# Q and K of the first band from rounded part and remainder, attention output per band, and a new order on all engines, in a fused window-attention block

## The reference

```python
h = roll(ln(x, g1, b1), (-3, -3), axis=(1, 2))
q, k, v = heads(window_partition(h) @ w_qkv + b_qkv)
attn = softmax(q * 32**-0.5 @ k.T + bias[rel_index] + shift_mask)
x = x + roll(window_reverse((attn @ v) @ w_proj + b_proj), (3, 3), axis=(1, 2))
return x + gelu(ln(x, g2, b2) @ w_fc1 + b_fc1) @ w_fc2 + b_fc2     # exact gelu
```

## Time and profile before

| | us |
|---|---|
| median of the three timed runs | 3138.68 |
| the profiled execution | 3140.98 |
| span of its trace, first to last instruction | 3139.2 |
| TensorE matmuls busy | 2989.0 (95%) |
| VectorE busy | 2907.3 (93%) |
| ScalarE busy | 2255.3 (72%) |
| GpSimd busy | 1385.2 (44%) |

### The profile page before, as it was taken

One profiled execution on the slowest core, in us unless ns is written; L12 is line 12 of the kernel. 1 busy time (PEld: TensorE's weight loads), 2 busy tenths in 40 slices (PEclk: granted clock), 3 DMA queues, 4 the chain that ended last, 5 costly groups with the idle time before them and its releaser, 6 DMA issues.

```text
span 3139.2 us, 119115 instructions
## 1 busy us (share of the span) xinstructions
PE 2989.0 (95%) x51984; PEld 2732.5 (87%) x51984; DVE 2907.3 (93%) x7463; ACT 2255.3 (72%) x4480; POOL 1385.2 (44%) x775
## 2 busy tenths in 40 slices
PE   5999999999999999999999999999999999999998
PEld 3888888988888888889888888988888898888887
DVE  7999999999999999999999999999999999999995
ACT  3777777777777777777777777777777777777775
POOL 2444444444444444444444444444444444444442
PEclk9999999999999999999999999999999999999999
DMA  1111111111111111111111111111111111111110
GB/s 54 33 33 33 33 43 33 33 40 37 33 35 42 33 33 33 44 33 33 40 37 33 33 43 34 33 33 44 33 33 42 35 33 33 40 36 34 33 28 22
DMA packets 217571, 111.78 MB, mean 36 GB/s; under 512 B 15095, under 2 KB 216791, under 8 KB 217047
## 3 DMA queue, kind: packets, MB, share of 16 engines
q1 hardware_dynamic: 216899, 104.14, 13.0%
q10 hardware_dynamic: 147, 0.02, 0.0%
HBM read 52.73 MB, written 51.38 MB: 33 GB/s over the span
## 4 chain that ended last, share of the span: by engine, by line
PE 59%; DVE 29%; ACT 9%; issue 3%; SPq 0%; DMA 0%; POOL 0%; POOLq 0%; DVEq 0%; ACTq 0%
PE psum L767 13%; PE psum L725 7%; DVE xn L556 7%; PE psum L692 6%; PE psum L727 5%; PE psum L726 5%; DVE scores L576 5%; PE psum L699 4%; PE psum L746 4%; PE psum L753 4%; PE psum L707 3%; PE psum L720 3%; PE psum L732 3%; ACT probs L356 3%; DVE stream L590 3%
## 5 line engine op out<-in xcount | busy, mean ns | idle before, releaser
L318 POOL TENSOR_TENSOR rstd<-ve,minus_half 112x7 f32<-112x7 f32 x256 | 380.3, 1486 | 1251.7 <-DVE ve L551 1251.7
L767 PE MATMUL psum<-wfc,hT 128*112 128x128 f32 x7168 | 803.5, 273 | 1.5 <-ACT hT L410 1.5
L767 PEld LDWEIGHTS psum<-wfc,hT 128*112 128x112 f32 x7168 | 791.2, 177 | 2.1 <-issue 2.1
L410 ACT ACTIVATE hT<-psum,bias_h 128x392 f32<-128x392 f32 x1024 | 573.7, 599 | 233.0 <-PE psum L727 232.9
L314 POOL TENSOR_TENSOR probs<-probs,row_inv 128x784 f32<-128x784 f32 x256 | 383.7, 1521 | 470.7 <-DVE row_inv L585 470.7
L576 DVE TENSOR_TENSOR scores<-scores,row_max 128x784 f32<-128x784 f32 x256 | 447.5, 1748 | 8.8
L725 PE MATMUL psum<-x2T_hi,wfc_hi 128*128 128x392 f32 x1024 | 405.6, 396 | 28.0 <-DVE stream L590 25.8
L590 DVE TENSOR_TENSOR stream<-psum,stream 112x384 f32<-112x384 f32 (+1 forms) x512 | 303.9, 602 | 97.2 <-PE psum L753 83.3
L556 DVE TENSOR_SCALAR xn<-stream,mean,rstd 112x128 f32<-112x128 f32 x896 | 375.4, 476 | 1.6 <-POOL rstd L318 1.6
L321 POOL TENSOR_TENSOR stream<-stream,brow_fc 112x896 f32<-112x896 f32 x128 | 360.3, 2815 | 5.6 <-DVE xn L556 5.6
L402 ACT ACTIVATE kT<-psum,bias_k 128x392 f32<-128x392 f32 x256 | 150.8, 589 | 289.0 <-PE psum L732 285.6
(11 more groups left out here) (77 smaller groups left out, 5785.4 us busy)
## 6 DMA issues: line engine op xcount, KB each, us to landing
x_in<-in_x SPq DMA_DIRECT2D x224, 168.0 KB
out<-stream SPq DMA_DIRECT2D x224, 168.0 KB
x_in<-in_x SPq DMA_DIRECT2D x224, 17.5 KB
out<-stream SPq DMA_DIRECT2D x224, 17.5 KB
x_in<-in_x SPq DMA_DIRECT2D x224, 10.5 KB
out<-stream SPq DMA_DIRECT2D x224, 10.5 KB
x_in<-in_x SPq DMA_DIRECT2D x32, 96.0 KB
out<-stream SPq DMA_DIRECT2D x32, 96.0 KB
```

The costliest lines, as they stand in the source:

```text
L410: act.activation(hT[:, chunk, band * BAND:(band + 1) * BAND], tok_psum(c)[:, 0:BAND], ACT.Gelu, bias=bias_h[:, chunk:chunk + 1]).then_inc( ...
L767: last = pe.matmul(tok_psum(h)[0:TOK, (t - t0) * C:(t - t0 + 1) * C], hT[:, chunk, t * TOK:(t + 1) * TOK], wfc2[:, chunk, :], start=chunk ...
```

## The change

It touches three things.

1. Q and K of band 0 are computed like those of band 1, by `product` on `xT_hi` and `xT_lo`, which now hold both bands. So `round_x(k, 0)` on ScalarE and `split_x(k, 0)` on VectorE are new, once per step.
2. `attend` and `copy_o` are split by band, each with its own semaphore; the output of band b lies at columns b*196 of both qkvo banks. The banks of V, Q and K change.
3. The order in every `step` is rewritten, with the waits that go with it, and some work moves to another n.

```diff
-xT_hi = sb("xT_hi", [C, 1, BAND], F32R)
-xT_lo = sb("xT_lo", [C, 1, BAND], F32R)
+xT_hi = sb("xT_hi", [C, 2, BAND], F32R)
+xT_lo = sb("xT_lo", [C, 2, BAND], F32R)
-V_BANK, Q_BANK, K_BANK = (1, 1), (0, 0), (0, 0)
+V_BANK, Q_BANK, K_BANK = (1, 0), (0, 1), (1, 0)
-def o_psum(parity):
-    return psum[:, QKVO_BANK + parity, 0:BANDS * PAIRS * N]
+def o_psum(band, parity):
+    return psum[:, QKVO_BANK + parity, band * PAIRS * N:(band + 1) * PAIRS * N]
...
-        act.activation(xT_hi[:, 0, :].rearrange("c (w n) -> c w n", n=N),
...
-        hi, lo = (part[:, 0, :].rearrange("c (w n) -> c w n", n=N) for part in (xT_hi, xT_lo))
+        hi, lo = (part[:, band, :].rearrange("c (w n) -> c w n", n=N) for part in (xT_hi, xT_lo))
...
-def copy_o():
+def copy_o(band):
+    image = oT[:, :, band, :].rearrange("c i (a w j) -> c w a i j", w=2, j=WIN)
-        for band in range(BANDS):
-            made = o_psum(parity)[:, band * PAIRS * N:(band + 1) * PAIRS * N]
-            image = oT[:, :, band, :].rearrange("c i (a w j) -> c w a i j", w=2, j=WIN)
-            last = act.activation(image[:, parity, :, :, :],
-                                  made.rearrange("c (a i j) -> c a i j", i=WIN, j=WIN), ACT.Copy)
-    last.then_inc(o_copied, 1)
+        last = act.activation(image[:, parity, :, :, :],
+                              o_psum(band, parity).rearrange("c (a i j) -> c a i j", i=WIN, j=WIN), ACT.Copy)
+    last.then_inc(o_copied[band], 1)
...
-def attend():
-    for band in range(BANDS):
-        for pair in range(PAIRS):
-            cols = slice((band * PAIRS + pair) * N, (band * PAIRS + pair + 1) * N)
-            for parity in range(2):
-                keys = slice(HALF * parity, HALF * parity + N)
-                for h in range(HEADS):
-                    rows = slice(HD * h, HD * (h + 1))
-                    last = pe.matmul(o_psum(parity)[rows, cols], vs[keys, band, pair, rows],
-                                     probsT[keys, band, h // 2, pair, h % 2, 0:N], start=True, stop=True)
-    last.then_inc(o_made, 1)
+def attend(band):
+    for pair in range(PAIRS):
+        cols = slice(pair * N, (pair + 1) * N)
+        for parity in range(2):
+            keys = slice(HALF * parity, HALF * parity + N)
+            for h in range(HEADS):
+                rows = slice(HD * h, HD * (h + 1))
+                last = pe.matmul(o_psum(band, parity)[rows, cols], vs[keys, band, pair, rows],
+                                 probsT[keys, band, h // 2, pair, h % 2, 0:N], start=True, stop=True)
+    last.then_inc(o_made[band], 1)
 def product(made, w_hi, w_lo, x_hi, x_lo):
 def qk_product(k, bank, part, band):
-    if band == 0:
-        return pe.matmul(made, wqk[:, part, :], xT[:, k % 2, 0, :, 0:N], start=True, stop=True)
-    return product(made, wqk_hi[:, part, :], wqk_lo[:, part, :], xT_hi[:, 0, :],
-                   xT_lo[:, 0, :])
+    return product(made, wqk_hi[:, part, :], wqk_lo[:, part, :], xT_hi[:, band, :],
+                   xT_lo[:, band, :])
 def make_q(k, band):
```

More of the change, by code:

```diff
@@ L336, in step @@
                     normalise_probs(1)
[L337 to L346, removed]
             run_steps(step)
@@ L419, in step @@
                 if has(n - 1):
+                    wait(act, fc1_made[5], upto(n - 1))
+                    gelu(5)
+                    wait(act, fc1_made[6], upto(n - 1))
+                    gelu(6)
+                if has(n):
+                    wait(act, o_made[1], upto(n))
+                    copy_o(1)
+                    copy_o(0)
+                if has(n - 1):
+                    wait(act, fc1_made[1], upto(n - 1))
+                    gelu(1)
                     wait(act, fc1_made[0], upto(n - 1))
                     gelu(0)
[L422 to L433, removed]
                 if has(n + 1):
@@ L436, in step @@
                     copy_q(1)
-                if has(n - 1):
-                    wait(act, fc1_made[5], upto(n - 1))
-                    gelu(5)
+                if has(n + 2):
+                    wait(act, xT_made[1], upto(n + 2))
+                    copy_x(n + 2, 1)
                 if has(n + 1):
@@ L644, in step @@
                     shift_scores(n, 1)
+                    wait(dve, exp_done[0], upto(n))
+                    inverse_sums(n, 0)
                 if has(n - 1):
@@ new lines, in step @@
+                if has(n - 1):
+                    wait(pe, gelu_done[5], upto(n - 1))
+                    make_hidden(1)
+                    wait(pe, gelu_done[6], upto(n - 1))
+                    make_hidden(0)
+                if has(n + 1):
+                    wait(pe, o_copied[0], upto(n))
+                    if n < 0:
+                        wait(pe, xT_split[1], upto(n + 1))
+                    make_q(n + 1, 1)
+                if has(n):
+                    wait(pe, gelu_done[1], upto(n - 1))
+                    project(1)
+                    wait(pe, gelu_done[0], upto(n - 1))
@@ L775, in step @@
                     project(0)
-                if has(n - 1):
+                if has(n + 2):
                     wait(pe, residual_added[1], upto(n))
-                    if n >= steps:
-                        wait(pe, gelu_done[3], upto(n - 1))
-                    make_hidden(5)
+                    if n < 0:
+                        wait(pe, xn1_ready[1], upto(n + 2))
+                    transpose_tiles(xn1, 1, xT_made)
                 if has(n + 1):
-                    wait(pe, q_copied[1], upto(n + 1))
@@ L793, in step @@
                     make_scores(1)
+                if has(n - 1):
+                    wait(pe, gelu_done[3], upto(n - 1))
+                    make_hidden(7)
                 if has(n + 2):
@@ L800, in step @@
                     transpose_tiles(xn1, 0, xT_made)
-                    wait(pe, gelu_done[7], upto(n - 1))
-                    transpose_tiles(xn1, 1, xT_made)
                 if has(n + 1):
@@ L805, in step @@
                 if has(n - 1):
+                    wait(pe, gelu_done[7], upto(n - 1))
+                    make_out(1)
                     wait(pe, xT_copied[0], upto(n + 2))
[L807 to L808 removed]
                     make_out(0)
[L810 to L814 removed]
```

235 lines of the change are left out of this document (98 added, 137 removed).

## The result

The changed kernel takes 3169.89 us against 3139.05 in the same comparison: ratio 1.0095, 95% interval 1.0078 to 1.0113. It is slower by 1%. The forecast was 3058 us and faster, with a range up to 3150.

The account below looks back on a forecast made before the run. TensorE was taken to bound the kernel, VectorE just under: 23.16 us at the granted clock, 0.12 gap and 0.10 joints made 23.38 a step; 127 steps plus 90 us gave 3059, adjusted to 3058; range 3022 to 3150.

Parts of the forecast that it names:

- TensorE's part: TensorE's own list per step: 22.86 us before plus 0.14 for the new arithmetic, 23.00 us.
- The gap: Idle matmul time in attend at instruction packet borders: 0.68 us a step before, 0.12 forecast after.
- a divide in the time of the 256 instructions ahead: In attend, a packet border stops TensorE if the 256 instructions ahead passed in under about 2.2 us.
- VectorE's clean list: VectorE's step without GpSimd meetings: 19.98 us plus 0.55 for the new split; 20.9 with the projection wait.
- The wait between the projections: VectorE between the two projections: an unavoidable 0.4 us, as half 0 takes longer than the addition of half 1.
- the sum of VectorE's meetings with GpSimd: Time VectorE loses per step where GpSimd excludes it: 0.8 to 2.3 us, leaving VectorE just under TensorE.
- `normalise` xn2 against `normalise_probs`: VectorE's unbroken xn2 run beside GpSimd's normalise_probs 0: 0 to 1.5 us, taken as 0.
- the 0.7 for xn1: VectorE's normalise xn1 against GpSimd's two add_rows: 0.2 to 1.6 us, taken 0.7.
- rival (c): GpSimd takes turns between tiles of VectorE's xn1 and xn2 runs: slower, 24.7 us a step, 3227 us; chance 0.2.
- my three signs of being wrong: VectorE's busy share passes TensorE's; single L556 rows reach 2 us mid-run; the L720 gap keeps its 73 us.
- the powers: GpSimd's rstd power, started by the first mean_var, against the second's small VectorE operations: 0 to 1.48 us.
- Slack of 2.5 us over a step: VectorE, 20.9 against 23.4 us a step, can lose 2.5 us to GpSimd and waits before it binds.

Follow-up runs that it names:

- adds_late: The changed kernel with both GpSimd add_rows of a step waiting until VectorE has normalised xn1; 3023.54 us, ratio 0.9653 to the kernel before.
- before_adds_late: The kernel before, old order and arithmetic, with GpSimd's add_row for x waiting until band 0's scores are shifted; 3114.91 us, ratio 0.9938.
- probs_late: The changed kernel with normalise_probs of band 0 waiting until VectorE has normalised xn2; 3105.42 us, ratio 0.9882 to the kernel before.

## Why the prediction was wrong

- **TensorE's part, 23.00 us: right**, in part by luck, as two small errors cancel. The undisturbed step of adds_late is 22.97. That of the old order without the late addition is 22.97 too (before_adds_late), where I had 22.86, and the 0.14 for the arithmetic did not show. L732 is gone as said.
- **The gap: right in size for this order**, 8.5 us left, or 0.07 a step against my 0.12. The packet border was right. The reason for its coming and going, a divide in the time of the 256 instructions ahead, was wrong: the place in `attend` separates, and what lies ahead sets how often and how long a late border stops the engine.
- **VectorE's clean list, 20.5 us plus waits: right.** 24.23 less 3.4 of meetings and 0.25 of waiting for an exponent is 20.6. The wait between the projections (0.4) did not occur, since VectorE came late to both.
- **The failed step** is the sum of VectorE's meetings with GpSimd, taken as 0.8: `normalise` xn2 against `normalise_probs`, "Value taken: 0", and with it the 0.7 for xn1, "If the second `add_row` slips in between tiles: 2.1 more", which I left to rival (c). Measured: 4.07 - 1.88 = 2.2 for xn1 and 2.02 - 0.85 = 1.2 for xn2, 3.4 in all where 2.57 had been before. With them VectorE needs 24.2 a step, more than TensorE's 23.0 and more than the 24.01 of before. I took the 0.08 us by which tiles overlap for an unbroken hold. The rows of before held the counter-evidence: `add_row` and L576 take turns at each border, and the tiles of xn1 and xn2 do the same. Two of my three signs of being wrong appeared, VectorE's share above TensorE's and single tiles of over 2 us within a run.
- **Rival (c) named mechanism, place and sign**; with 24.7 it was too dear by 0.5. Its full sum of 25.3 had 2.8 for xn1 (2.2 measured), 1.5 for xn2 (1.2) and 0.4 between the projections (none); the powers, which it added in some steps, delayed nobody. Its chance of 0.2 was too low, and the range left it out.
- **The joints.** Slack of 2.5 us over a step was also the wrong test. In probs_late VectorE has lost only the 2.2 of xn1, less than 2.5, and the step is still 23.71. The 2.2 falls into the one stretch ahead of the residual addition, for which TensorE waits 1.3 in every step of the changed kernel. The 1.2 at xn2 lies elsewhere, and taking it away gave 0.51.

## What to carry to other kernels

Where GpSimd and VectorE exclude each other, count every GpSimd instruction that becomes ready during a run of short VectorE instructions at its full length: it gets in after the one that is running. Two GpSimd instructions back to back cost most here, as the second was ready after the very first tile. One wait that moves them beside VectorE instructions that GpSimd does not hold up, here the readers of PSUM and the reductions (0.97 us each beside `add_row` in adds_late, as alone), is worth trying first: it gave 1.14 us of a step of 24.22. And sum an engine's losses per stretch between two places where engines wait for each other, not per step.

## What the runs showed of the hardware that I had not expected

The rstd powers do not exclude VectorE: L575, with two inputs in SBUF, took 0.97 us though it started beside the second power (both powers are in the row 1517.62 to 1520.59), and did so in all 125 cases; the small operations of `mean_var` took 0.16 to 0.17 us beside the first. The spans of GpSimd are rough in this profile, so for how much of its row the power holds memory is not known. The Trainium skill ("SBUF — State Buffer", SBUF: two separate sides) would have such a VectorE operation blocked for the whole GpSimd instruction; here the measurement decides.

A hold ends with one instruction, also between two tiles that overlap by 0.08 us: GpSimd's second `add_row` came in behind a single tile. The Trainium skill says in the same section that whichever starts first "gets the pair for the whole instruction"; the trace agrees, with a tile of 2.14 us beside an `add_row` of 2.12.
